# Second buffers, own slots and a repeating restack for the stacks of attention b; Newton steps in three pieces

## The reference

```python
x = x + attn_a(layernorm(x))   # 16 heads of 8, latent keys and values, causal softmax
x = x + ffn(layernorm(x))      # r * (relu(xk @ W_k)**2 @ W_v), xk and xr mix x with its left neighbour
x = x + attn_b(layernorm(x))   # 16 heads of 8, q and k of each head scaled to length 1, scores * 8, causal
x = x + ffn(layernorm(x))      # the same weights
```

## Time and profile before

| | us |
|---|---|
| median of 3 runs | 1287.57 (1280.78 to 1295.53) |
| the profiled execution | 1295.43 |
| its span | 1293.7 |
| mean granted TensorE clock, share of full | 0.891 |

### The profile page before, as it was taken

How to read it: one execution, slowest core, us unless ns; L and a number is a source line. 1 busy time by engine, 2 the same in 40 slices (tenths; PEclk the granted TensorE clock), 3 DMA queues, 4 the chain that set the end, 5 groups by cost and what they waited for, 6 DMA issues and landing times.

```text
span 1293.7 us, 43418 instructions
## 1 busy us (share of the span) xinstructions
PE 1039.2 (80%) x19057; PEld 591.0 (46%) x19057; DVE 872.4 (67%) x2068; ACT 787.2 (61%) x1026; POOL 273.5 (21%) x260
## 2 busy tenths in 40 slices
PE   3357786898888888888889888898889888897865
PEld 2114343454554454454555444455455445554533
DVE  6448576777688676868678586868777687764412
ACT  2025464676766576666667576666767677686742
POOL 2011122222223121312222031222212131213112
PEclk9558688898999898999889899889989899899877
DMA  1541344342717053261707144271806134124130
GB/s 29 107 107 55 56 109 99 92 107 68 158 34 172 19 143 66 92 125 59 158 19 176 24 130 87 67 149 35 181 13 173 36 122 87 60 52 107 46 63 17
DMA packets 86061, 113.33 MB, mean 88 GB/s; under 512 B 13040, under 2 KB 79728, under 8 KB 79728
## 3 DMA queue, kind: packets, MB, share of 16 engines
q1 hardware_dynamic: 85872, 110.55, 36.6%
HBM read 55.22 MB, written 54.53 MB: 85 GB/s over the span
## 4 chain that ended last, share of the span: by engine, by line
PE 45%; DVE 28%; ACT 11%; issue 9%; DMA 5%; POOL 1%; SPq 1%; POOLq 0%; DVEq 0%; ACTq 0%
PE acc L613 14%; DVE rowmax L970 10%; PE pool L592 7%; ACT prob L813 5%; PE pool L531 4%; DVE xn L928 3%; PE pool L497 3%; PE pool L562 2%; DVE ssum L1048 2%; DMA stack_qb<-scratch_qb 2%; PE pool L625 2%; DMA stack_qa<-scratch_qa 2%; DVE step_r L1068 2%; PE pool L653 2%; PE pool L639 2%
## 5 line engine op out<-in xcount | busy, mean ns | idle before, releaser
L813 ACT ACTIVATE prob<-pool 128x1024 f32<-128x1024 f32 x576 | 568.1, 1026 | 305.7 <-PE pool L599 301.7
L970 DVE TENSOR_REDUCE rowmax<-pool 128x2 f32<-128x1024 f32 (+7 forms) x480 | 360.9, 793 | 229.3 <-PE pool L537 229.1
L613 PE MATMUL acc<-prob,vals_a 128*32 128x512 f32 (+7 forms) x2048 | 190.2, 465 | 7.5 <-issue 7.5
L531 PE MATMUL pool<-stack_ka,stack_qa 48*64 48x512 bf16 (+7 forms) x2048 | 134.2, 317 | 75.6 <-DVE rowmax L970 40.0
L599 PE MATMUL pool<-mask_t,ident_b 64*64 64x64 bf16 x4096 | 169.1, 198 | 12.7 <-issue 12.7
L592 PE MATMUL pool<-stack_qb,stack_kb 48*64 48x512 bf16 (+7 forms) x2048 | 125.2, 303 | 54.0 <-DVE rowmax L970 28.0
L613 PE MATMUL acc<-prob,vals_b 128*32 128x512 f32 (+7 forms) x2048 | 158.2, 415 | 0.0
L531 PEld LDWEIGHTS pool<-stack_ka,stack_qa 48*64 48x64 bf16 x2048 | 63.5, 113 | 186.5 <-issue 97.3
L592 PE MATMUL pool<-stack_qa,stack_ka 51*64 51x512 bf16 (+7 forms) x2048 | 122.1, 312 | 21.5 <-DVE rowmax L970 11.3
L599 PEld LDWEIGHTS pool<-mask_t,ident_b 64*64 64x64 bf16 x4096 | 124.9, 113 | 13.5 <-issue 13.5
L592 PEld LDWEIGHTS pool<-stack_qb,stack_kb 48*64 48x64 bf16 x2048 | 60.7, 109 | 116.4 <-DVE rowmax L970 37.5
(11 more groups left out here) (133 smaller groups left out, 1477.2 us busy)
## 6 DMA issues: line engine op xcount, KB each, us to landing
stack_qa<-scratch_qa SPq DMA_DIRECT2D x32, 384.0 KB, 6.5
stack_ka<-scratch_ka SPq DMA_DIRECT2D x32, 384.0 KB, 9.4
stack_kb<-scratch_kb SPq DMA_DIRECT2D x32, 384.0 KB, 11.1
stack_qb<-scratch_qb SPq DMA_DIRECT2D x32, 384.0 KB, 13.9
scratch_qa<-parts_q SPq DMA_DIRECT2D x16, 384.0 KB, 2.6
scratch_ka<-parts_k SPq DMA_DIRECT2D x16, 384.0 KB, 2.6
scratch_qb<-parts_q SPq DMA_DIRECT2D x16, 384.0 KB, 2.6
scratch_kb<-parts_k SPq DMA_DIRECT2D x16, 384.0 KB, 3.0
```

Source lines behind the costliest of these rows:

```text
L531: eng.matmul(ps[half:half + BLK, k, at:at + w], queries[rows, pair, BLK * blk:w], keys[rows, pair, 0:w], start=True, stop=False)
L613: last = eng.matmul(acc[32 * j:32 * j + 32, BLK * blk:T], vals[a][:, blk, GROUP * g + j, :], prob[n % NPROB][:, k, at:at + T - BLK * blk], ...
L813: eng.activation(prob[n % NPROB][:, :, :], place["unit", n][0][:, :, :], ACT.Exp, scale=scale).then_inc(S["exped"], 1)
L970: last = eng.tensor_reduce(to, of, axis=AX.X, op=ALU.max)
```

## The change

Attention b's stacks get a second buffer. Its restacks leave the end of the b attention before and get slots of their own, 116 for k and 121 for q (shifted with the rest of the middle where that is compressed), not earlier than 72 slots before attention b. `split` writes each part once: one DMA of 384 KB in place of three with 768 KB. `restack` makes the repetition: for each half r and each entry of `STACK` one DMA, six in place of two, whose DRAM source has the dimensions [copies or parts, 8 rows, 4096 elements], with a step of 0 in the first one where a part is repeated. `written_` counts 16 a stack, `stacked_` 96. `rsqrt` yields after each Newton step, at slots 91, 94 and 97.

```diff
-    "middle_back": [73, 79, 83, 90, 90, 91, 107, 109, 113],
+    "restack_b": [116, 121],
+    "middle_back": [73, 79, 83, 90, 90, 91, 94, 97, 107, 109, 113],
...
-        stack = {n: [sb(f"stack_{n}{i}", [P, PAIRS, T], BF16) for i in range(2 if n[1] == "a" else 1)]
+        stack = {n: [sb(f"stack_{n}{i}", [P, PAIRS, T], BF16) for i in range(2)]
...
-        scratch = {n: nc.dram_tensor("scratch_" + n, (PRODUCTS, P, T), BF16, kind="Internal").ap()
+        scratch = {n: nc.dram_tensor("scratch_" + n, (3, P, T), BF16, kind="Internal").ap()
...
             for k, n in enumerate("kq"):
-                yield e.restack(b, n, "b"), [max(back[-1] + 3 + k, end_b)]
+                slot = PLAN["restack_b"][k] - PLAN["middle_back"][-1] + back[-1]
+                yield e.restack(b, n, "b"), [max(slot, of_b - 2 * SLOTS + k)]
...
                     eng.scalar_tensor_tensor(rnorm[:, :], step_r[:, :], 1.5, rnorm[:, :], ALU.add,
                                              ALU.mult).then_inc(S["newton"], 1)
-                yield
+                    yield
...
             def split(self, b, n, a):
-                eng, q = self.eng, self.q
-                for first, *chosen in STACK:
-                    c = chosen[0 if n == "q" else 1]
-                    src = (parts[n][:, c[0]:c[0] + 1, :].to_broadcast([P, len(c), T]) if c[0] == c[-1]
-                           else parts[n][:, 0:len(c), :])
-                    q.wait_ge(S[f"stacked_{n}{a}"], 32 * b)
-                    q.wait_ge(S[f"part2_{n}{a}"], b + 1)
-                    eng.dma_start(scratch[n + a][first:first + len(c)].rearrange("t r c -> r t c"),
-                                  src).then_inc(S[f"written_{n}{a}"], 16)
+                eng, q = self.eng, self.q
+                q.wait_ge(S[f"stacked_{n}{a}"], STACKED * b)
+                q.wait_ge(S[f"part2_{n}{a}"], b + 1)
+                eng.dma_start(scratch[n + a].rearrange("t r c -> r t c"),
+                              parts[n][:, :, :]).then_inc(S[f"written_{n}{a}"], 16)
...
                 for r in range(2):
-                    src = scratch[n + a].rearrange("t (d r a) c -> (t d) r (a c)", d=D, r=2)[:, r, :]
-                    eng.dma_start(to[BLK * r:BLK * r + ROWS, :, :].rearrange("p a c -> p (a c)"),
-                                  src).then_inc(S[f"stacked_{n}{a}"], 16)
+                    for first, *chosen in STACK:
+                        c = chosen[0 if n == "q" else 1]
+
+                        step = 0 if c[0] == c[-1] else P * T
+                        src = bass.AP(scratch[n + a].tensor, c[0] * P * T + r * PAIRS * T,
+                                      [[step, len(c)], [2 * PAIRS * T, D], [1, PAIRS * T]])
+                        row = BLK * r + D * first
+                        eng.dma_start(to[row:row + D * len(c), :, :].rearrange("p a c -> p (a c)"),
+                                      src).then_inc(S[f"stacked_{n}{a}"], 16)
```

More of the change, by code:

```diff
@@ L19 @@
 NPROB = 4
-PRODUCTS = 6
 STACK = [(0, (0, 0, 0), (0, 1, 2)), (3, (1, 1), (0, 1)), (5, (2,), (0,))]
+STACKED = 16 * 2 * len(STACK)
 SLOTS = 36
@@ L515, in row_maxima @@
                 eng, q = self.eng, self.q
-                q.wait_ge(S["stacked_qa"], 32 * (b + 1))
-                q.wait_ge(S["stacked_ka"], 32 * (b + 1))
+                q.wait_ge(S["stacked_qa"], STACKED * (b + 1))
+                q.wait_ge(S["stacked_ka"], STACKED * (b + 1))
                 queries, keys = stack["qa"][b % 2], stack["ka"][b % 2]
@@ L580, in attend @@
                         q.wait_free(freed)
-                        q.wait_ge(S[f"stacked_q{a}"], 32 * (b + 1))
-                        q.wait_ge(S[f"stacked_k{a}"], 32 * (b + 1))
+                        q.wait_ge(S[f"stacked_q{a}"], STACKED * (b + 1))
+                        q.wait_ge(S[f"stacked_k{a}"], STACKED * (b + 1))
                         if a == "a":
@@ L763, in split @@
                 a_, b_ = split_before[n, a, b]
-                q.wait_ge(S[f"written_{n}{a_}"], 48 * (b_ + 1))
+                q.wait_ge(S[f"written_{n}{a_}"], 16 * (b_ + 1))
                 q.wait_ge(S[f"projected_{n}{a}"], b + 1)
@@ L1301, in restack @@
                     q.wait_ge(S["scored"], unit_of[a, b_][-1] + 1)
-                q.wait_ge(S[f"written_{n}{a}"], 48 * (b + 1))
+                q.wait_ge(S[f"written_{n}{a}"], 16 * (b + 1))
                 for r in range(2):
-                    src = scratch[n + a].rearrange("t (d r a) c -> (t d) r (a c)", d=D, r=2)[:, r, :]
-                    eng.dma_start(to[BLK * r:BLK * r + ROWS, :, :].rearrange("p a c -> p (a c)"),
-                                  src).then_inc(S[f"stacked_{n}{a}"], 16)
+                    for first, *chosen in STACK:
[6 more added lines that the diff above has]
+                                      src).then_inc(S[f"stacked_{n}{a}"], 16)
                 yield
```

## The result

The changed kernel takes 1399.33 us (median of four runs, 1392.36 to 1403.37). The kernel before, run beside it, takes 1291.55 (1280.78 to 1296.92). The ratio is 1.084, 95% interval 1.075 to 1.093: slower, by twice the forecast.

What follows compares the result with a forecast made beforehand. No engine is full; in-order TensorE's stops lengthen the run, so transfers must stay hidden. Terms +40+15+14-16 = +53 on the profiled 1295.4 gave 1349, or 1341 relative to the median 1287.6; range 1250 to 1425 us.

Steps and rivals of the forecast that it cites:

- the engines of each form: Repeating restacks: q's DMAs on 3, 2 and 8 engines, 34 rows on engine 0; k joined, 8 rows.
- Landing of ka: One line on engine 0 from the maxima's issue: qb 11.4, write 1.1, qa 11.4, x_in 0.7, ka 2.7, about 2 extra.
- Price of a row: An 8 KB row on one DMA engine takes 0.334 us (24.5 GB/s); bounds 0.30 to 0.71 us.
- Rival C: One engine really moves only 11.5 GB/s: q takes 24 us, each period +28, about 1600 us; chance 0.05.
- What this does to a period: Steady periods: stacks land late at the row maxima, +5.2 us at batch 7, mean +3.6 over 11 periods, +40.
- Clock and Newton between the stops: Slow clock behind the row-maxima stops, 1.5 us ten times, +15; Newton in pieces, -1.2 us in 13 periods, -16.
- Own slots: b's restack slots: no gain in the steady-period sum; leaving a's crowd counted only in rival A.
- rival A: Lowering finds 12 or more engines for q; unexplained stops lose half, -25; about 1238 us, faster; chance 0.12.
- Start and end: First batches +4, +4, +3, first b stack +3; last two b stacks -2 and +2; together +14.
- Writes: SyncE saves 1.1 us a write, pays four more issues of 0.4 a restack; 0, bounds 0 and +3 a period.
- B: k is not joined either: 34 rows for k too, +129 in 11 periods, ends +52, about 1522 us; chance 0.08.
- D: Transfers stay just hidden, rows at 0.30 us or less: within 1%, about 1295 us; chance 0.15.

Runs made afterwards that it cites:

- e13: The changed kernel with the six ka restack DMAs moving 512 B of each 8 KB row from batch 5 on: 1345.35 us, ratio 1.043.
- e5: The kernel before with only the Newton steps split into three pieces: 1267.79 us, ratio 0.978.
- e6: The kernel of e3 with the Newton steps in one go again: 1241.66 us, ratio 0.959.
- e11: The kernel before with only second buffers for b's stacks; slots, writes, restacks and Newton as before: 1288.64 us, ratio 0.997.
- e7: The kernel before with second buffers and own slots for b's stacks; writes, wide restacks and Newton as before: 1255.90 us, ratio 0.970.
- e1: The changed kernel with six products written and 48 rows restacked by one DMA a half, as before: 1227.09 us, ratio 0.952.
- e3: The changed kernel with the restack source's two outer dimensions swapped, rows outermost; same bytes, DMAs and slots: 1212.83 us, ratio 0.942.
- e4: The changed kernel with b's restacks moved late, behind a's restacks and the group-1 maxima; copies still outermost: 1250.02 us, ratio 0.971.
- e10: The changed kernel with rows outermost in the restack source and b's restacks late, behind the group-1 maxima: 1198.22 us, ratio 0.926.
- e2: The kernel before with only the repeating restack, copies outermost; one b buffer, old slots, Newton in one go: 1471.27 us, ratio 1.143.

## Why the prediction was right and wrong

Right: the direction, the place (L536 behind stack_ka, 11 times), the engines of each form (q on 3, 2 and 8, k joined), and the range. The median came out at +108 us where +53 was forecast. On the spans it is +101.4: +23 by the row maxima of batch 4 (304.30 against 281.01 us), +73 to those of batch 15 (1180.88 against 1084.30), +5 behind. The forecast had +14 for the start and end, and +39 between. (1295.4 + 53 is 1348, not 1349; nothing hangs on it.)

- **Landing of ka, the term that failed: the two q stacks were costed too low.** 29.3 us were forecast from the end of the maxima's issue. In after it is 34.7 (507.54 to 542.23). The trace's semaphore events split it, at batch 7: qb has landed after 16.2 us, where 1 + 11.4 was forecast; the ka write 1.0 later (forecast 1.1); qa 14.2 later (forecast 11.4); x_in 0.8 later (0.7); ka 2.6 later (2.7 and 1 for landing). So the write and x_in were sized right and ka 1 us too high; the excess is in qb and qa, 3.8 and 2.8 us. The mean over the eleven periods is 34.7 too, with 15.7 for qb and 14.7 for qa.
- **Price of a row: right for narrow DMAs alone, wrong in company.** 0.334 us was forecast for each of q's 34 rows, and 0.31 is read at 532 to 536 us in after, where nothing else moves. Rival C (0.71) is false. But the step took the engines of a narrow DMA to be undisturbed. The kb restack (500.15) and the qa write (504.15) are still moving when qb starts, 175 GB/s at a share of 0.71 at 504 to 508, 15 GB/s an engine; kb ends 0.4 us and the qa write 1.9 us behind the maxima's issue. And beside ka the rows go at 152 GB/s at 0.80, 12 an engine. e13 shows the size of that: with ka's rows nearly empty, qa lands 11.1 us behind the ka write at batch 7, close to the 11.4 forecast, and not 14.2. For qb no run separates what is waiting in line from what is a slower row. The Trainium skill, page "DMA: Bandwidth & Descriptors", section "Specifications", gives about 27 GiB/s an engine; the 26.5 GB/s read here is 9% under it. With the page's figure the prediction's estimate of the sum was about +5, further off.
- **What this does to a period.** At batch 7 the road from the maxima's issue to the row maxima grew by 37.8 - 27.1 = 10.7 us, forecast 5.2. The mean over the eleven periods was forecast at +3.6; it is +9.2 (37.8 against 28.7): +101 us instead of +40.
- **Clock and Newton between the stops.** Forecast +15 - 16 = -1. The rest of the period, from the row maxima to the next maxima issue, shrank from 44.4 us to 41.9: -28. The stops at L536 do put the clock to 0.50, as the step said, but the period between gained more: Newton is worth 22 to 27 us (e5, e6), not 16, because a stop of 2 us often costs clock afterwards.
- **Own slots: taken as nothing, worth about -35 with the wide restack.** They pull b's stacks out of the crowd of four, and the "issue" stops fall from 38.0 to 22.3 us (e11, e7). The forecast had seen this, but only in rival A, at -25. In after the gain can't be seen by itself, for the row maxima start right behind ka's landing (542.23, 542.37) whatever TensorE saved ahead of it. Without the narrow restacks the change was a gain of 4.8% (e1); the narrow form cost 13 to 14 per cent of before's time (after against e1 and e3), some 170 to 185 us, where the sum had 69.
- **Start and end.** The stops ahead of the row maxima of batches 0, 1 and 2, which the profile books as "issue", are 16.8, 8.8 and 5.8 us before and 24.5, 16.8 and 13.4 in after: +23, where +4, +4 and +3 were forecast. The first stacks were forecast complete at 51.0 us; qa alone landed at 37.45 + 14.96 = 52.4. The last two qb landings hold the chain for 13.6 and 12.7 us, before 9.1 and 10.1; "not gone" was right. Forecast were -2 and +2, nothing together; it was +5.
- **Writes.** Right: 1.57 us for three issues became 0.38 for one, and nobody gained. But the step's "four more issues of 0.4 a restack" was wrong under load: six issues took 5.22 us, x_in's one 2.53, and the group-1 maxima 8.43 instead of 2.95.

That the measured time lies in the stated range is partly luck: the road to the row maxima was forecast 61 us too short in the sum, the start 9 (14 with the first b stack, against 23) and the end 5, but the rest of the periods 27 too long. Errors of opposite sign made the forecast look closer than it was.

**Rivals.** A did not happen: q ran on 3, 2 and 8 engines. Kernels with 16 or 8 engines for q, e1 and e3, took 1227 and 1213 us, where A had 1238. B is excluded by the packets, C by the price of a row. D had rows of 0.30 us as its condition; they cost 0.31 alone, and the stacks landed late all the same, because they were not alone.

## What to carry to other kernels

Where a DMA's source repeats, put the rows outermost and the copies inside: the same six DMAs went from 1.084 to 0.942 by two swapped dimensions. When costing a chain of narrow DMAs, count all that is still moving when it starts and all that will move beside it: a row at 0.31 us alone made 11 us of a q stack, in company 14 to 16. Ask separately what each other part of the change is worth: the slots were booked at nothing and gave 35 us, Newton at 16 and gave 22 to 27. A critical transfer should not stand behind an uncritical one in its queue; e4 and e10 gained 0.113 and 0.016 by moving two restacks.

## What the runs showed of the hardware that was not expected

- A DMA engine moved 8 KB rows at 26.5 GB/s when only two were working (after, 532 to 536 us), and at 10 to 12 when all 16 were writing restacks (172 GB/s at 1.03 in e11).
- Rows of a DMA went slower beside those of a DMA issued behind it: qa took 14.2 us behind the ka write with full ka rows beside it, 11.1 with 512 B ones (after and e13, batch 7).
- Issuing a DMA took longer while narrow DMAs were under way: four 6 KB DMAs took 2.96 us in one place and 8.43 (after) or 11.27 (e2) in another. That their queue was full is likely, not shown.
- A stop of TensorE of 2.05 us was followed by 4 us at a granted clock of 0.61, a stop of 1.19 us at the same place by 1.00 (e6 and e3). It was so in 12 and in none of 13 periods; in before, with 2.05 us too, in 8 of 13.
- TensorE stopped for 1.7 to 4.9 us with no semaphore waited for, in before and e11 only behind a DMA share of about 1.0; in e7 some such stops of 1.2 to 1.8 us stood behind shares of 0.56 to 0.65. With 8 engines a restack they nearly vanished (0.5 us in e3). All of them over 1 us, 21 in before and e11, ended 1.2 to 1.6 us behind a packet of the instruction queue. The cause is argued, not shown.
